# Second attention of a fused transformer kernel: readers of a shared PSUM bank between pairs of row maxima, its visits placed anew, and the layer normalisation on GpSimd

## The reference

```python
x = x + 0.5 * L0_ffn(layernorm(x))      # 4 experts, top 1
x = x + L0_attn(layernorm(x))
x = x + 0.5 * L0_ffn(layernorm(x))
x = x + 0.5 * L1_ffn(layernorm(x))      # 32 experts, top 4
x = x + L1_attn(layernorm(x))           # the layer of the change
x = x + 0.5 * L1_ffn(layernorm(x))
```

```python
qkv = (x @ w_qkv).reshape(B, L, 3, 16, 8)       # q, k, v
q, k = rope(q), rope(k)
attn = softmax(einsum('bhqd,bhkd->bhqk', q, k) * 8 ** -0.5)
out = einsum('bhqk,bhkd->bhqd', attn, v)        # back to (B, L, 128)
return out @ w_proj + b_proj
```

## Time and profile before

| | us |
|---|---|
| median of 3 runs | 2680.11 (2675.53 to 2683.67) |
| the profiled execution's own time | 2689.33 |
| its span, first to last instruction | 2687.6 |
| TensorE busy in the span | 2304.1 (86%) |
| VectorE | 2038.6 (76%) |
| ScalarE | 1321.5 (49%) |
| GpSimd | 927.6 (35%) |
| mean granted TensorE clock, share of full | 0.921 |

### The profile page before, as it was taken

One profiled execution on the slowest core, in us unless ns is written; L12 is line 12 of the kernel. 1 busy time (PEld: TensorE's weight loads), 2 busy tenths in 40 slices (PEclk: granted clock), 3 DMA queues, 4 the chain that ended last, 5 costly groups with the idle time before them and its releaser, 6 DMA issues.

```text
span 2687.6 us, 39104 instructions
## 1 busy us (share of the span) xinstructions
PE 2304.1 (86%) x11234; PEld 1569.8 (58%) x11234; DVE 2038.6 (76%) x4733; ACT 1321.5 (49%) x1911; POOL 927.6 (35%) x836
## 2 busy tenths in 40 slices
PE   4499467769589999949999999999999996999999
PEld 3377356547477777725545454545554553787777
DVE  6588577658489999847777777777777774888887
ACT  0188222258444444425555555555555554444444
POOL 6600666410267777621111111111111100556554
PEclk9999555579789999959999999999999998999999
DMA  6343111044188888911111111111111111788897
GB/s 163 102 134 113 35 34 32 20 134 153 53 184 173 178 183 172 191 46 51 56 52 53 52 51 51 51 51 51 51 51 51 54 52 32 165 185 177 177 188 156
DMA packets 142703, 265.92 MB, mean 99 GB/s; under 512 B 21004, under 2 KB 24079, under 8 KB 142335
## 3 DMA queue, kind: packets, MB, share of 16 engines
q1 hardware_dynamic: 134174, 247.44, 38.5%
q0 software_dynamic: 8416, 17.25, 2.5%
HBM read 212.44 MB, written 54.27 MB: 99 GB/s over the span
## 4 chain that ended last, share of the span: by engine, by line
PE 59%; DVE 14%; issue 10%; ACT 7%; DMA 6%; SPq 2%; POOL 1%; POOLq 1%; DVEq 0%; ACTq 0%
PE ps L1863 12%; PE ps L1887 9%; PE ps L1607 7%; PE ps L1609 7%; PE ps L1608 7%; PE ps L1874 6%; DMA gate_rows<-gates_dram 4%; DVE shift L1485 3%; DVE m L1322 2%; ACT g L809 2%; PE ps L1621 1%; ACT g_hi L782 1%; PE ps L1936 1%; PE ps L1614 1%; PE ps L1634 1%
## 5 line engine op out<-in xcount | busy, mean ns | idle before, releaser
L1485 DVE TENSOR_REDUCE shift<-ps 128x1 fp32r<-128x512 f32 x1024 | 670.8, 686 | 122.8 <-PE ps L1863 120.8
L927 ACT ACTIVATE prob<-ps 128x1024 f32<-128x1024 f32 x512 | 522.4, 1025 | 411.3 <-PE ps L1874 403.9
L782 ACT ACTIVATE hi<-m 128x512 fp32r<-128x512 f32 x512 | 318.9, 631 | 414.9 <-DVE m L1322 414.8
L1863 PE MATMUL ps<-k_pad,q_st 128*128 128x512 f32 x1024 | 418.8, 451 | 81.5 <-DVE shift L1485 65.9
L628 POOL TENSOR_TENSOR lo<-m,hi 128x512 fp32r<-128x512 f32 x256 | 341.4, 1335 | 308.2 <-ACT hi L782 307.5
L1322 DVE SCALAR_TENSOR_TENSOR m<-ps,gate_rows 128x512 f32<-128x512 f32 x512 | 335.3, 681 | 91.5 <-PE ps L1609 47.0
L1863 PEld LDWEIGHTS ps<-k_pad,q_st 128*128 128x128 f32 x1024 | 181.6, 191 | 370.5 <-DVE shift L1485 329.2
L1874 PE MATMUL ps<-q_sh,k_pad 128*128 128x512 f32 x1024 | 329.1, 403 | 0.0
L1887 PE MATMUL ps<-prob,v_cols 128*32 128x512 f32 x2048 | 275.8, 611 | 0.4 <-ACT prob L927 0.4
L604 POOL TENSOR_SCALAR var_eps<-meanvar 128x4 f32<-128x4 f32 x48 | 11.1, 230 | 675.0 <-DVE meanvar L1041 674.0
L1006 DVE TENSOR_TENSOR lo<-m,hi 128x512 fp32r<-128x512 f32 x256 | 208.5, 815 | 16.4
(11 more groups left out here) (213 smaller groups left out, 3949.4 us busy)
## 6 DMA issues: line engine op xcount, KB each, us to landing
gate_rows<-gates_dram SPq DMA_DIRECT2D x256, 512.0 KB, 6.5
w_blk<-w_dram SPq DMA_DIRECT2D x38, 514.5 KB, 3.7
q_st<-q_dram SPq DMA_DIRECT2D x64, 256.0 KB, 2.6
k_dram<-qk_hl SPq DMA_DIRECT2D x48, 256.0 KB, 3.0
q_dram<-qk_hl SPq DMA_DIRECT2D x48, 256.0 KB
k_pad<-k_dram SPq DMA_DIRECT2D x256, 48.0 KB
x_blk<-sorted_x SPq DMA_DIRECT2D x38, 256.0 KB, 3.5
sorted_y<-yb_rows SPq DMA_DIRECT2D x38, 256.0 KB, 2.0
```

The source lines that it names most:

```text
L782: return act.activation(o, i, ACT.Copy)
L927: act.activation(prob[:, h % HP, 2 * half:2 * half + 2, :], ps[:, b0:b0 + 2, :], ACT.Exp, scale=SCALE).then_inc(sig(ph, "prob"), 1)
L1485: dve.tensor_reduce(shift[:, g % 2, b, c:c + 1], wide(PASS1 + b % 2), AXX, ALU.max, negate=True).then_inc(sig(ph, "qmax"), 1)
L1863: pe.matmul(wide(PASS1 + b % 2), q_st[:, g % 2, b * P:b * P + P], k_pad[:, HPG * g + j], start=True, stop=True).then_inc(sig(ph, "s1"), 1)
```

## The change

The shared bank's visits get new places, its readers on VectorE all go between maxima 1 and 2, and the normalisation of phase 4 goes to GpSimd.

- TensorE: input transposes early in step 0; v late in 0; q/k 0 to 3 late in 1, 3, 4 and 5; shifts early in 3, 7, 11 and 15, as before; the last output transposes of the tile before late in 7, attended late in 8, the projection late in 9; output transposes 0 to 2 late in 11, 12 and 13. The middle place is gone.
- VectorE: rotary 0 to 3 in steps 2, 4, 5 and 6; the last output of the tile before in 8, the added projection in 10, outputs 0 to 2 in 12 to 14. The statistics are taken for the tile after the next one, `bn_stats` of two blocks each at the end of steps 11 and 12, the aggregation at the end of 13. It no longer normalises.
- ScalarE: the copies of the transposes, of v and of the attended transposes stand between the two exponentials of steps 0, 1 and 9; the roundings of q and k (`rope_high`) ahead of those of 5 and 7.
- GpSimd: root and normalisation (`apply_norm4`, the form of phases 3 and 5) for the tile after the next, then that tile's low parts and sums, and the bias last. Its head does so for tiles 0 and 1.
- `EARLY` goes from 9 to 11.

Removed runs of more than three lines are left out of the diff; they stand in the functions above.

```diff
@@ -39,7 +39,7 @@
 CHUNKS = 4
 PER_CHUNK = FB1 // CHUNKS
 AHEAD = 5
-EARLY = 9
+EARLY = 11
 FIRST = (0, 0, TILES, 0, 0, TILES)
 KIND = (0, 1, 0, 3, 4, 3)
...
@@ -746,31 +746,46 @@
                         pool.tensor_tensor(qk_hl[:, a, 1], rope[:, 2], qk_hl[:, a, 0].bitcast(F32),
                                            ALU.subtract).then_inc(sig(4, "qk_hl"), 1)
-                    def ahead4(t, p, first=False):
-
+                    def apply_norm4(t, first=False):
+                        pass_wait(pool, sig(4, "rstd"), t + 1)
                         if not first:
-                            bias(t)
+                            pass_wait(pool, sig(4, "tr"), t)
+                        xt = x[:, bass.ds(t * BLK, BLK), :]
+                        every = [P, BLK, D]
+                        pool.tensor_tensor(xn[:], xt, meanvar[:, :, 0:1].broadcast_to(every),
+                                           ALU.subtract).then_inc(sig(4, "centred"), 1)
+                        pool.wait_ge(sig(4, "centred"), t + 1)
+                        pool.tensor_tensor(xn[:], xn[:], rstd[:].unsqueeze(2).broadcast_to(every),
+                                           ALU.mult).then_inc(sig(4, "xn"), 1)
+                    def ahead4(t, p):
                         x_low(t, p)
                         for a in range(2):
                             rope_sum(t, a)
                             rope_low(t, p, a)
+                        bias(t)
                     def head4(t, p):
                         rstd_of(4)(t, p)
-                        pool.wait_ge(sig(4, "xn"), t + 1)
+                        apply_norm4(t, True)
                         pool.memset(shift[:].bitcast(F32), 0.0).then_inc(sig(4, "zeroed"), 1)
                         for b in range(2):
                             pool.memset(v_cols[b][:, :, :, HD + 1:VC], 0.0)
                             last = pool.memset(v_cols[b][:, :, :, HD:HD + 1], 1.0)
                         last.then_inc(sig(4, "zeroed"), 1)
                         pool.wait_ge(sig(4, "tables"), 16 * 5)
-                        ahead4(t, p, True)
-                        bias(t)
+                        ahead4(t, p)
+                        rstd_of(4)(t + 1, 1 - p)
+                        apply_norm4(t + 1)
+                        ahead4(t + 1, 1 - p)
                     def body4(t, p, more):
-                        if more:
-                            rstd_of(4)(t + 1, 1 - p)
-                            ahead4(t + 1, 1 - p)
+                        if two_more(t):
+                            rstd_of(4)(t + 2, p)
+                            apply_norm4(t + 2)
+                            ahead4(t + 2, p)
                     over_tiles(pool, 4, head4, body4)
                 barrier(pool, ph + 1)
@@ -943,18 +958,16 @@
                         o_out(before, GROUPS - 1)
                     if h in (5, 9, 13):
                         o_out(t, (h - 5) // HPG)
+                    if h in (5, 7) and more:
+                        rope_high(n, q, (h - 5) // 2)
                     exps(t, h, 0)
-                    if h == 6 and more:
-                        rope_high(n, q, 0)
-                    if h == 12 and more:
+                    if h == 0 and more:
+                        head_a(n, q)
+                    if h == 1 and more:
                         head_b(n, q)
+                    if h == 9 and before is not None:
+                        project(before)
                     exps(t, h, 1)
...
@@ -1504,13 +1510,13 @@
                                       ALU.mult).then_inc(sig(ph, "o_all"), 1)
                 def head(t, p):
-                    normalise(ph, t, 0)
-                    normalise(ph, t, 1)
+                    normalise(ph, t)
                     for n in range(GROUPS):
                         last = dve.memset(k_pad[:, HPG * n:HPG * n + HPG].bitcast(F32), 0.0)
                     last.then_inc(sig(ph, "zeroed"), 1)
                     for i in range(4):
                         rotary(t, i)
+                    normalise(ph, t + 1)
                     dve.wait_ge(sig(ph, "zeroed"), 3)
                     for h in range(AHEAD):
                         if h == HPG:
@@ -1525,38 +1531,51 @@
                     dve.tensor_tensor(x_tile(ph, t), x_tile(ph, t), rows4(MISC), ALU.add)\
...
-                def step(t, p, h, more, before=None):
+                def moments_of(t, blocks):
+                    if blocks[0] == 0:
+                        dve.wait_ge(sig(ph, "xn"), t)
+                        pass_wait(dve, sig(3, "x_done"), t * 4 + 4)
+                    for b in blocks:
+                        last = dve.bn_stats(stats[:, b, :], x_block(ph, t, b))
+                    if blocks[-1] == BLK - 1:
+                        last.then_inc(sig(ph, "stats"), 1)
+                def moments_done(t):
+                    pass_wait(dve, sig(ph, "stats"), t + 1)
+                    for b in range(BLK):
+                        last = dve.bn_aggr(meanvar[:, b, :], stats[:, b, :])
+                    last.then_inc(sig(ph, "meanvar"), 1)
+                def step(t, p, h, more, before=None, two_on=False):
                     n = t + 1
...
                     ahead = h + AHEAD
                     if ahead < HEADS or more:
                         maxima(t + ahead // HEADS, ahead % HEADS // HPG, ahead % HPG, (0, 1))
...
+                    if h in (2, 4, 5, 6) and more:
+                        rotary(n, (2, 4, 5, 6).index(h))
                     if h in (3, 7, 11):
                         shifted_queries(t, (h + 1) // HPG)
                     if h == 15 and more:
                         shifted_queries(n, 0)
+                    if h == 8 and before is not None:
+                        output(before, GROUPS - 1)
+                    if h == 10 and before is not None:
+                        add_projected(before)
+                    if h in (12, 13, 14):
+                        output(t, h - 12)
                     if ahead < HEADS or more:
                         maxima(t + ahead // HEADS, ahead % HEADS // HPG, ahead % HPG, (2, 3))
...
+                    if two_on and h in (11, 12):
+                        moments_of(t + 2, (2 * (h - 11), 2 * (h - 11) + 1))
+                    if two_on and h == 13:
+                        moments_done(t + 2)
                 def body(t, p, more):
                     for h in range(EARLY, HEADS):
-                        step(t, p, h, more)
+                        step(t, p, h, more, two_on=two_more(t))
                     if more:
                         for h in range(EARLY):
                             step(t + 1, 1 - p, h, two_more(t), before=t)
@@ -1939,73 +1958,56 @@
                 def early_work(t, p, h, more, before):
                     n, q, g4 = t + 1, 1 - p, t * GROUPS
+                    if h == 0 and more:
+                        bank_read("qsh_sb", g4 + 1)
+                        transpose_in(ph, n, MISC)
                     if h == 3:
-                        if before is not None:
-                            bank_read("oT_sb", before + 1)
+                        if more:
+                            bank_read("qk_read", n * 4 + 1)
                         else:
                             bank_read("qsh_sb", g4 + 1)
                         shifted(t, 1, p)
-                    if h == 6 and more:
-                        bank_read("qk_read", n * 4 + 2)
-                        head_qk(n, q, 2)
                     if h == 7:
                         if more:
                             bank_read("qk_read", n * 4 + 4)
                         else:
                             bank_read("qsh_sb", g4 + 2)
                         shifted(t, 2, p)
...
                     if h == 11:
-                        bank_read("o_all", g4 + 2)
                         shifted(t, 3, p)
-                    if h == 12 and more:
-                        bank_read("qsh_sb", g4 + 4)
-                        head_v(n, q)
                     if h == 15 and more:
                         bank_read("o_all", g4 + 3)
                         shifted(n, 0, q)
...
                 def late_work(t, p, h, more, before):
                     n, q, g4 = t + 1, 1 - p, t * GROUPS
...
+                    if h == 0 and more:
+                        bank_read("x_hi", n + 1)
+                        head_v(n, q)
+                    if h == 1 and more:
+                        bank_read("v_cols", n + 1)
+                        head_qk(n, q, 0)
                     if h == 3 and more:
                         bank_read("qsh_sb", g4 + 2)
...
+                        head_qk(n, q, 1)
+                    if h in (4, 5) and more:
+                        bank_read("qk_read", n * 4 + h - 2)
+                        head_qk(n, q, h - 2)
+                    if h == 7 and before is not None:
+                        bank_read("qsh_sb", g4 + 3)
+                        o_rows(before, GROUPS - 1)
```

(67 more changed lines are left out.)

52 lines of the change are left out of this document (7 added, 45 removed).

## The result

The changed kernel takes 2569.76 us (median of 4 runs, 2560.17 to 2572.57), the kernel before 2679.98 on the same occasion: ratio 0.9583, 95% interval 0.9554 to 0.9612. That is 110 us less; 96 were forecast, and 2569.76 lies 0.24 us under the range's lower end of 2570. A second series gave 2569.98 and 0.9594 (0.9573 to 0.9615).

The account below looks back on a forecast made before the run. Neither TensorE nor VectorE is full; their waiting order (pair, maximum 0, TensorE) bounds. Tiles 1 to 14 92.4, tile 0 5.8, head 2.7, jumps -5: 96 us off 2680.1 gives 2584, range 2570 to 2612.

Parts of the forecast that it names:

- The steps: Second attention: each new step priced by an old step with the same visit and reader; sum 57.8 us a tile against 64.55.
- VectorE's idle time before maximum 0: Sign in steps with readers on VectorE: idle under 0.4 us before the step's first maximum.
- The statistics: bn_stats behind maximum 3 of steps 11 and 12 cost nothing, the aggregation behind 13 some 0.2 us a tile; ends 0 and 1.38.
- The moved waits: Waits of v, q/k products, roundings and the next tile's q load keep their margins; taken at nothing.
- Rival 1: A margin fails: v, q/k 0 or a rounding waits for ScalarE or GpSimd, 1 to 3 us a tile, 2600 to 2630; chance 0.13.
- Rival 2: VectorE becomes the bound in steps 11 to 14, 3.77 against 3.48 us: 18 us, 2602; chance 0.09.
- Rival 3: xn from GpSimd comes late for the transposes in slot 0; 2697 if GpSimd's 4.5 us become 15; chance 0.04.
- Rival 4: The price of a visit is hidden in its neighbour, so half the gain comes: 2632; chance 0.04.
- The jump: Loop jump between steps 10 and 11: maximum 0 at 3.0 us, 0.8 us more in each of six jumps, 5 us; ends 0 and 12.
- I keep such falls as they are: Falls to the lower clock after a jump, up to 1.7 us lost in tile 2, left unchanged in the sum.
- tile 0: First tile of the second attention, without three of the visits: 5.8 us gained by the same steps.
- Head and end: Head of the phase gains 2.7 us as VectorE's k_pad memsets start right behind the moments; tile 15 and drain 0.

Follow-up runs that it names:

- experiment 6: Changed kernel with nine of the 13 VectorE readers (rotary, output, added projection) ahead of maximum 0 again, visits as changed: 2729.80 us, ratio 1.0173.
- experiment 7: Kernel before with only five VectorE readers (three outputs, rotary 0 and 3) moved behind maximum 1: 2623.02 us, ratio 0.9781.
- experiment 8: Changed kernel with q/k 3 early in step 5 instead of late, so two visits share a slot: 2587.61 us, ratio 0.9651.
- experiment 1: Kernel before with only EARLY changed from 9 to 11, moving the loop's jump: 2676.52 us against 2683.51, ratio 0.9979.
- experiment 3: The burst: changed kernel with three added 256 KB copies issued by SyncE in every tile after step 10's first score matmuls: 2580.47 us, median of two runs.
- experiment 4: Changed kernel with EARLY 12 and the statistics one step later: 2583.31 us against 2569.98 for the changed kernel on the same occasion.
- experiment 9: Changed kernel with the normalisation back on VectorE, behind step 14 and in the head; GpSimd makes the root only: 2577.59 us, ratio 0.9608.

## Why the prediction was right and where it was not

**The steps.** "Each combination has a step in the earlier trace rows, so a tile is priced by them" held to 0.02 us for every kind but the projection (3.94 for 3.98): the odd tiles take 57.7 to 57.8 against 57.8 without the statistics. Experiments 6, 7 and 8 show the chain behind it from three sides. A reader ahead of maximum 0 costs 1.1 to 1.3 us, behind maximum 1 nothing (3.48 with an output's reader in step 8, 3.48 with none in step 9); a second visit in a slot costs 1.2 us. One sign was off: VectorE's idle time before maximum 0, forecast under 0.4 us, is 0.41 to 0.74 in tile 5, except behind the statistics.

**The statistics.** The 0.2 us for the aggregation were not paid: steps 12 to 14 take 3.48 in the odd tiles. That is 14 x 0.2 = 2.8 us.

**The moved waits** cost nothing, as taken: from tile 1 on no step is over 3.95 outside the jumps. GpSimd's xn came in time. The q load was priced to go out 8.7 us after the start of step 7; in tile 5 it goes out after 6.8, so its margin was larger than the 2 us worked out:

```profile
1529.91 0.35 SPq L557 DMA_DIRECT2D q_st<-q_dram  x1
```

Rivals 1 to 3 fell by the signs given for them: no step over 4.3, steps 12 to 14 not at 3.8, one wait for xn in the head only. Rival 4 (half the gain) fell by the time.

**The jump is the step that failed**, in two terms. "If it comes at 3.0" took over from step 9 the 3.1 us after the pair at which VectorE resumed, and priced a jump 0.8 us dearer, 5 us in all; and "I keep such falls as they are" left the clock's falls in. Measured: maximum 0 comes at 2.12, and a jump without a fall costs 1.55 us where it cost 1.87; and in this profile no fall follows a jump, where four did, at 1.6 us each. That makes -1.9 and -6.3, so -8.2 where +5 stood: 13.2 us of the 14.3 by which the 15 tiles came out better than forecast. The rest is the statistics (-2.7) against tile 0 (58.8 us, 1.5 more than forecast: its first two steps take 4.51 and 4.69, and the clock is at its lower level for the first 5.5 us of them). The bounds set for the jump, 0 and 12 us dearer, didn't hold the measured value either; cheaper jumps stood only at the foot of the whole range.

The cause of VectorE's empty time is shown by experiments 1, 3 and 4: it ends at a fixed time after one packet of instructions starts, and this packet moves on the same 16 DMA engines as the q save and the k loads. The jump at step 9 stood in their traffic; the one at step 11 stands beside none. The prediction had the pieces. It moved the q load, which closes this traffic, 3.4 us earlier and the jump two steps later, but used the load for its own margin alone and never laid the two side by side.

**The clock.** The rule of the Trainium skill weighed in the prediction ("TensorE: Matmul & The Clock Gate", Part 1), that the slow clock is the default and activity lifts it, points the right way, and the trace agrees so far: the falls went with TensorE's wait at the jump, 1.28 us in tile 4 against 2.69. The eleven profiles with a loop have 66 jumps. None of the 38 with a wait of TensorE up to 1.46 us was followed by a fall, three of the four with 1.51 to 1.65 were (two of them in experiment 9), all six of the burst (1.8 to 2.2), all six of experiment 4 (2.3 to 2.5), but only three of six in experiment 7 (2.2 to 2.3) and four of six in the kernel before (2.65 to 2.7). So a longer wait made a fall likelier, but its length alone doesn't decide; what else does stays open. So the 6.3 us are a matter of the jumps' place and partly of chance: one fall came back in the changed kernel's second profile.

**Head and end.** 2.7 forecast, 3.3 measured (2.7 by experiment 9). Tile 15 was taken at 0: its steps are cheaper too, and it brought 2.7. With the 3.3 us outside the phase the profiles differ by 20.8 us more than the 96 forecast; 6.6 of them are there because the kernel before was profiled 9.4 us above its median and the changed one 2.8 above. The other 14.2 are the miss.

**The other rule** of the Trainium skill, of "SBUF — State Buffer", says that VectorE and GpSimd shut each other out only where VectorE reads two SBUF operands or runs in a two-port mode. The trace agrees so far as it goes: GpSimd is busy 161.9 us in the 15 tiles instead of 134.4, its two normalising instructions (columns as in the page) take 1.04 us each, not the 1.37 of the earlier trace rows, and the maxima keep their 0.68.

```profile
L756 POOL TENSOR_TENSOR xn<-x,meanvar 128x512 f32<-128x512 f32 x14 | 14.6, 1043 | 5.6 <-POOL rstd L606 5.6
L759 POOL TENSOR_TENSOR xn<-xn,rstd 128x512 f32<-128x512 f32 x14 | 14.6, 1040 | 1.1
```

## What to carry to other kernels

Where two engines hand small buffers back and forth, read one period of it from the trace, name the chain, and put every other reader where the chain's partner is busy anyway; then spread the visits so that none waits inside a period for another's reader. Price a moved piece by a step that already has the same pieces in the same order. A loop's jump can need a transfer of instructions, as VectorE's did here: look for an engine's empty time after its branch, put the jump where the DMA engines are quiet when that packet is due, or write the loop out where the program may grow.

## What the runs showed of the hardware that was not expected

- After a jump VectorE had no instruction for 2.8 us with quiet DMA engines and up to 4.0 with other transfers in flight; the 8 KB packet started 1.0 and 2.0 to 2.2 us after the branch. One 256 KB load at the wrong moment (28.0% of the engines' time in 3 us) did as much harm as a queue that took 92.5%.
- ScalarE, GpSimd and TensorE had their next instruction 0.05 to 0.3 us after their branches in the same loop. Why is open. Between two branches of the changed kernel the trace has 336 instructions on VectorE, 168 on ScalarE, 43 on GpSimd and over 1500 on TensorE, so their number alone doesn't sort the engines. The trace has a second instruction queue, with packets of 16 KB. It moves 8 of them in the 15 tiles of the changed kernel and none across the six jumps, but 39 when the loop is written out. Which engines it serves, the trace doesn't say.
- Written out, seven times as many instructions of the phase's loop came without a gap: 57.7 to 57.85 us in each of tiles 1 to 14.
- A stretch of 3.4 us at the lower clock after a jump cost 1.6 us in the kernel before (tile 2 68.0 against 66.4 in tile 4, with the same empty time on VectorE). In the changed kernel's second series tile 2 took 61.2 against 59.3, and part of these 1.9 us is a packet that started 0.3 us later.
